# A recommendation tower on one core: a new order of each chunk's work on TensorE, ScalarE and VectorE

## The reference, cut to what matters

```python
e = jnp.stack([tbl_f[ids[:, f]] for f in range(26)], axis=1)      # 2048 x 26 x 128
combined = concatenate([dense[:, None, :], e], axis=1)            # 27 vectors of a sample
inter = einsum('bnd,bmd->bnm', combined, combined)[:, triu_i, triu_j]   # 351 products
h = concatenate([dense, inter, dense], axis=1)                    # 607 features
h = maximum(h @ W_top1 + b_top1, 0)                               # 512
h = maximum(h @ W_top2 + b_top2, 0)                               # 256
y = h @ W_top3                                                    # 2048 x 1
```

## Time and profile before

| | before |
|---|---|
| device time, median of 3 runs | 371.46 us |
| device time of the profiled execution | 371.68 us |
| its span | 369.8 us |
| TensorE busy with matmuls | 331.2 us (90%) |
| GpSimd busy | 259.1 us (70%) |
| VectorE busy | 208.4 us (56%) |
| ScalarE busy | 188.2 us (51%) |
| mean granted TensorE clock | 0.991 |

### The profile page before, as it was taken

How to read it: one execution, slowest core, us unless ns; L and a number is a source line. 1 busy time by engine, 2 the same in 40 slices (tenths; PEclk the granted TensorE clock), 3 DMA queues, 4 the chain that set the end, 5 groups by cost and what they waited for, 6 DMA issues and landing times.

```text
span 369.8 us, 13491 instructions
## 1 busy us (share of the span) xinstructions
PE 331.2 (90%) x6048; PEld 295.2 (80%) x6048; DVE 208.4 (56%) x376; ACT 188.2 (51%) x222; POOL 259.1 (70%) x280
## 2 busy tenths in 40 slices
PE   0486759899999999999999989998999989999797
PEld 0476747898899889997899769996889868997676
DVE  3799925792289506980398406980289505960031
ACT  2698643356355664556365554555445552555402
POOL 6777777777777777777777777777777777777100
PEclk9999998999999999999999999999999999999989
DMA  7999527672236512672247322572236512542330
GB/s 178 249 256 206 159 69 236 141 228 56 60 78 171 169 51 62 124 232 60 54 96 194 127 58 54 125 241 51 58 85 158 176 52 53 110 111 59 77 47 14
DMA packets 49332, 44.24 MB, mean 120 GB/s; under 512 B 33359, under 2 KB 39094, under 8 KB 49274
## 3 DMA queue, kind: packets, MB, share of 16 engines
q1 hardware_dynamic: 39166, 25.36, 27.4%
q0 software_dynamic: 8704, 17.84, 18.0%
q10 hardware_dynamic: 1404, 0.17, 0.3%
HBM read 37.91 MB, written 5.44 MB: 117 GB/s over the span
## 4 chain that ended last, share of the span: by engine, by line
PE 78%; DMA 8%; POOL 4%; issue 4%; SPq 2%; ACT 2%; DVE 0%; DVEq 0%
PE banks L449 37%; PE banks L472 13%; PE mlp L492 8%; PE moved L431 8%; PE mlp L502 7%; DMA hidden<-in_tbl_dram 6%; POOL rows L404 4%; DMA rows<-in_tbl_dram,ids_sb 3%; SPq L253 2%; PE banks L538 1%; PE mlp L514 1%; PE banks L552 1%; ACT vectors L866 1%; ACT vectors L849 1%; PE mlp L538 1%
## 5 line engine op out<-in xcount | busy, mean ns | idle before, releaser
L404 POOL DMA_INDIRECT rows<-in_tbl_dram,ids_sb x272 | 258.1, 949 | 83.9 <-issue 80.2
L711 DVE TENSOR_TENSOR masks<-hot_ids,row_of 125x512 fp32r<-125x512 int32 (+1 forms) x336 | 186.4, 619 | 59.9 <-PE banks L449 51.6
L449 PE MATMUL banks<-masks,high 125*128 125x256 f32 x592 | 152.4, 296 | 16.7 <-DVE low L698 16.7
L449 PE MATMUL banks<-masks,low 125*128 125x256 f32 x592 | 147.2, 287 | 0.0
L449 PEld LDWEIGHTS banks<-masks,high 125*128 125x128 f32 x592 | 115.6, 195 | 17.7 <-issue 14.6
L449 PEld LDWEIGHTS banks<-masks,low 125*128 125x128 f32 x592 | 115.9, 196 | 0.0
L866 ACT ACTIVATE vectors<-moved 128x512 f32<-128x512 f32 (+1 forms) x79 | 86.5, 1094 | 22.6 <-PE moved L431 22.6
L849 ACT ACTIVATE vectors<-banks 128x512 f32<-128x512 f32 (+1 forms) x40 | 44.4, 1110 | 70.4 <-PE banks L449 70.4
L472 PEld LDWEIGHTS banks<-vectors 128*27 128x27 f32 x4096 | 45.6, 104 | 22.6 <-issue 14.8
L472 PE MATMUL banks<-vectors 128*27 128x27 f32 x4096 | 56.3, 193 | 4.7 <-issue 3.7
L431 PE MATMUL moved<-identity,rows 128*128 128x128 f32 x271 | 45.0, 281 | 14.1 <-ACT vectors L866 6.4
(11 more groups left out here) (49 smaller groups left out, 65.4 us busy)
## 6 DMA issues: line engine op xcount, KB each, us to landing
hot_ids<-in_ids_of_field_dram SPq DMA_DIRECT2D x32, 256.0 KB, 4.7
rows<-in_tbl_dram,ids_sb POOLq DMA_INDIRECT x272
features<-scratch SPq DMA_DIRECT2D x7, 351.0 KB
scratch<-products SPq DMA_DIRECT2D x56, 42.2 KB
scratch<-products SPq DMA_DIRECT2D x28, 81.2 KB
w_sb<-in_tbl_dram SPq DMA_DIRECT2D x3, 448.0 KB
hot_ids<-in_ids_of_field_dram SPq DMA_DIRECT2D x8, 128.0 KB
dense_sb<-in_dense_dram SPq DMA_DIRECT2D x8, 128.0 KB, 5.3
```

Of the source, the lines that this page charges most:

```text
L404: pool.indirect_dma_start(rows[:, (tile * TILE_ROWS + v) % RING, :], None, tables[f][:, :], bass.IndirectOffsetOnAxis(ap=ids_sb[:, tile, f ...
L449: last = nc.tensor.matmul(banks[:, j % BANKS, m * CHUNK:(m + 1) * CHUNK], part[:, part_of(j * PAIR + m, k), :], masks[:, mask % MASK_RING, ...
L711: nc.vector.tensor_tensor(masks[:, mask % MASK_RING, 0:size], hot_ids[0:PART_ROWS, n % ID_RING, 0:size], row_of[0:PART_ROWS, row:row + 1]. ...
```

## The change

On TensorE a chunk now has this order: the turns of tile a stand between `look_up(i, 2)`, `look_up(i, 3)`, `look_up(i, 4)` and `first_layer(i-1, 0)`. Behind the last of them come steps 0 and 1 with the rest of the first layer and two turns of tile b, then the whole second layer, then `look_up(i+1, 0)` and the first two masks of `look_up(i+1, 1)` between the later turns of tile b, and last the visits of steps 2 and 3 with the rest of `look_up(i+1, 1)` between them. So two lookups of the next chunk, not one, run ahead of it. In `end` the last layers of chunk 6 stand ahead of the last turn, and two of half 0's four first-layer tiles stand between steps 2 and 3. ScalarE's and VectorE's queues are put in the matching order. On SyncE's queue the store of chunk 6's results moves ahead of the last writes.

The diff, with TensorE's part whole but for `first_chunk`, and the rest cut:

```diff
             def chunk(i):
-                a = TILES * i
+                a, b = TILES * i, TILES * i + 1
                 turn(a, 0)
-                look_up(i, 1)
+                look_up(i, 2)
                 last_layer(i - 2)
                 turn(a, 1)
-                look_up(i, 2)
+                look_up(i, 3)
                 turn(a, 2)
-                look_up(i, 3)
+                look_up(i, 4)
                 turn(a, 3)
-                look_up(i, 4)
+                first_layer(i - 1, 0)
                 turn(a, 4)
-                if i < LAST:
-                    end_of_chunk(i)
-
-            def end_of_chunk(i):
-                b = TILES * i + 1
-                first_layer(i - 1, 0)
+                if i == LAST:
+                    return
                 multiply(i, 0, (0,))
-                turn(b, 0)
                 first_layer(i - 1, 1)
                 multiply(i, 0, (1,))
-                turn(b, 1)
+                turn(b, 0)
                 first_layer(i - 1, 2)
                 multiply(i, 1, (0,))
+                first_layer(i - 1, 3)
+                multiply(i, 1, (1,))
+                turn(b, 1)
+                second_layer(i - 1, 0)
+                second_layer(i - 1, 1)
                 turn(b, 2)
-                first_layer(i - 1, 3)
+                look_up(i + 1, 0)
                 turn(b, 3)
-                multiply(i, 1, (1,))
-                second_layer(i - 1, 0)
+                look_up(i + 1, 1, range(0, 2))
                 turn(b, 4)
-                second_layer(i - 1, 1)
-                multiply(i, 2, (0,))
-                look_up(i + 1, 0, range(0, 3))
-                multiply(i, 2, (1,))
-                look_up(i + 1, 0, range(3, 5))
-                multiply(i, 3, (0,))
-                look_up(i + 1, 0, range(5, PARTS[0]))
-                multiply(i, 3, (1,))
+                products_of_second_tile(i)
+
+            def products_of_second_tile(i):
+                multiply(i, 2, (0,))
+                look_up(i + 1, 1, range(2, 4))
+                multiply(i, 2, (1,))
+                look_up(i + 1, 1, range(4, 6))
+                multiply(i, 3, (0,))
+                look_up(i + 1, 1, range(6, PARTS[1]))
+                multiply(i, 3, (1,))
...
             def end():
...
-                second_layer(LAST - 1, 0, range(2, MTILES1))
+                last_layer(LAST - 1)
                 turn(b, 4)
-                second_layer(LAST - 1, 1, range(0, 2))
                 multiply(LAST, 2)
-                multiply(LAST, 3)
-                second_layer(LAST - 1, 1, range(2, MTILES1))
-                last_layer(LAST - 1)
                 first_of_half(0, 0, every)
                 first_of_half(0, 1, every)
+                multiply(LAST, 3)
                 first_of_half(0, 2, every)
                 first_of_half(0, 3, every)
...
         # VectorE
                 make_masks(i, 0)
+                make_masks(i, 1)
                 place_dense(i)
-                make_masks(i, 1)
                 keep_dense(i - 1)
...
         # SyncE
             write_last(0)
             load_last(0)
+            store_y(LAST - 1)
             write_last(1)
-            store_y(LAST - 1)
             load_last(1)
```

More of the change, by code:

```diff
@@ L580, in end @@
                 multiply(LAST, 1, (1,))
+                turn(b, 1)
+                first_layer(LAST - 1, 3)
+                second_layer(LAST - 1, 0)
                 turn(b, 2)
[L582 to L583 removed]
+                second_layer(LAST - 1, 1)
                 turn(b, 3)
[L585 removed]
+                last_layer(LAST - 1)
                 turn(b, 4)
[L587 removed]
                 multiply(LAST, 2)
[L589 to L591 removed]
                 first_of_half(0, 0, every)
                 first_of_half(0, 1, every)
+                multiply(LAST, 3)
                 first_of_half(0, 2, every)
@@ L617, in first_chunk @@
                 turn(1, 1)
-                multiply(0, 0)
+                multiply(0, 0, (0,))
                 turn(1, 2)
-                multiply(0, 1)
+                multiply(0, 0, (1,))
                 turn(1, 3)
+                multiply(0, 1, (0,))
+                look_up(1, 0, range(0, 3))
+                multiply(0, 1, (1,))
+                look_up(1, 0, range(3, PARTS[0]))
                 turn(1, 4)
-                multiply(0, 2, (0,))
-                look_up(1, 0, range(0, 3))
@@ L625, in first_chunk @@
-                multiply(0, 2, (1,))
-                look_up(1, 0, range(3, 5))
-                multiply(0, 3, (0,))
-                look_up(1, 0, range(5, PARTS[0]))
-                multiply(0, 3, (1,))
-            def second_chunk():
-                turn(2, 0)
-                look_up(1, 1)
-                turn(2, 1)
-                look_up(1, 2)
-                turn(2, 2)
-                look_up(1, 3)
-                turn(2, 3)
-                look_up(1, 4)
-                turn(2, 4)
-                end_of_chunk(1)
+                look_up(1, 1, range(0, 2))
@@ L683, in _ @@
             pe.wait_ge(constants_made, CONSTANTS)
             first_chunk()
-            second_chunk()
-            for i in range(2, CHUNKS):
+            for i in range(1, CHUNKS):
                 chunk(i)
@@ L986, in chunk @@
             def chunk(i):
-                a = TILES * i
+                a, b = TILES * i, TILES * i + 1
                 keep_batch(a, 0)
-                keep_pair(i, 1)
+                keep_pair(i, 2)
                 keep_y(i - 2)
                 keep_batch(a, 1)
-                keep_pair(i, 2)
+                keep_pair(i, 3)
                 keep_batch(a, 2)
-                keep_pair(i, 3)
+                keep_pair(i, 4)
                 keep_batch(a, 3)
-                keep_pair(i, 4)
+                keep_first(i - 1, 0)
@@ L997, in chunk @@
                 keep_batch(a, 4)
-                if i < LAST:
-                    end_of_chunk(i)
-            def end_of_chunk(i):
-                b = TILES * i + 1
-                keep_first(i - 1, 0)
-                keep_batch(b, 0)
+                if i == LAST:
+                    return
                 keep_first(i - 1, 1)
                 keep_step(i, 0)
+                keep_batch(b, 0)
+                keep_first(i - 1, 2)
+                keep_first(i - 1, 3)
+                keep_step(i, 1)
@@ L1029, in end_of_last @@
                 keep_batch(b, 2)
-                keep_first(LAST - 1, 3)
+                keep_second(LAST - 1, 0)
                 keep_batch(b, 3)
-                keep_second(LAST - 1, 0)
             first_chunk()
-            second_chunk()
-            for i in range(2, CHUNKS):
+            for i in range(1, CHUNKS):
                 chunk(i)
```

40 lines of the change are left out of this document (13 added, 27 removed).

## The result

The changed kernel takes **398.88 us** (median of 4 runs, 395.53 to 400.89) against 371.50 us before: a ratio of 1.072 with a 95% interval of 1.069 to 1.075. It is slower by 27 us. The forecast was 397 us, slower, with a range of 384 to 410.

The account below looks back on a forecast made before the run. Gathers (42.6 us a chunk) bound the old kernel; the loop through DRAM, 14.3 + 30.2 = 44.5 us, would bind the new. With start and end the time was 391.3 us, plus 5.8 for low clock: 397 us, range 384 to 410.

Parts of the forecast that it names:

- loop through DRAM: Product step, drain, writes, load, first layer, next product step: claimed to set each chunk's cycle at 44.5 us.
- Rivals 1 and 4: 1: faster, gathers keep the lead, 370.6 us, chance 0.04; 4: no effect, time stays at 371.5 us, chance 0.02.
- rival 2: The way through DRAM stays hidden, the drain waits do not: cycle 42.85 us, time 381 us, chance 0.08.
- rival 3: All goes badly: 15.1 us for the way, low clock in all seven chunks; 407 us, with beyond chance 0.14.
- The way: Products through DRAM, from a chunk's last product step to the landed load: 14.3 us, within 13.5 and 15.1.
- The wait for the load: TensorE ahead of each chunk's first layer: 1.65 us a chunk, 0.85 to 2.45.
- (a): Step 0, right behind the turn of tile a's last batch, waits for ScalarE's drain: 1.0 us a chunk.
- (b): Chunk's end: a lookup's drain stands ahead of tile b's fourth batch's, so the next turn waits: 0.85 us.
- (c): Step 2 waits for ScalarE's drain of the last batch: 0.75 us a chunk.
- From the first layer to the next step 3: TensorE's stretch from first-layer start to the next chunk's last product step: 23.5 us before, 30.2 us after, drain waits included.
- The clock: TensorE at low clock behind waits: 4.2 us over half of seven chunks, plus 1.6 us at the end.
- The end: After the last load: 24.3 us to the last product step, half 0's load binding, then 10.2 and 7.7 us.

Follow-up runs that it names:

- x_way: Changed kernel, but in chunks 1 to 6 only half of the products are written to DRAM and loaded back, TensorE's instructions unchanged; 388.55 us.
- x_twice: Kernel before the change, but each chunk's products except the last's are written to DRAM twice before the load; 415.71 us.
- x_drain: Changed kernel with TensorE and ScalarE work reordered to remove its three waits for ScalarE's drains; 387.41 us.
- x_hold: Changed kernel with useless matmuls (5, 3, 4, 1 and 20) where TensorE waits, each filling meant to be shorter than its wait; 393.22 us.
- x_chunk: Changed kernel with the old end of the program, so only the chunks have the new order; 393.52 us.
- x_tail: Kernel before the change with only the new end of the program; 375.37 us.
- x_load: Changed kernel with half of the next chunk's second lookup moved behind the chunk's last product step; 391.03 us.
- x_even: Changed kernel reordered to remove the load wait and the three drain waits, with step visits and other work alternating; 381.01 us.
- x_both: Changed kernel with the edits of x_load and x_drain together; 382.13 us.
- x_best: Kernel before the change with another end: second-layer work between the last chunk's last two product steps; 370.44 us against 371.22, ratio 0.998.

## Why the prediction was right

**The bound.** Right. The loop through DRAM took the gathers' place in every chunk; x_way (a shorter way, same instructions) and x_twice (a longer one in the old order) show it from both sides. Rivals 1 and 4 fell with the waits for rows that never came back, rival 2 with the 9.8 us of waits for loads, and rival 3 needed 15.1 us of way and a low clock in every chunk.

**The way.** 14.3 us were taken, within 13.5 and 15.1. Measured from the end of step 3 to the first layer: 13.5 to 14.65 us, 14.0 on average. In the chain above the tile starts 0.04 us behind the landing.

**The wait for the load.** 1.65 us a chunk; measured 0.85 to 2.0, 1.40 on average, 9.8 us in seven. The way's excess over the 12.65 us of TensorE's work was the right sum.

**The waits for ScalarE.** (a) 1.0 was taken, 0.83 measured; (b) 0.85 and 1.1; (c) 0.75 and 0.51. Their sum, 2.4 us against 2.6, and their places are right, as the chain shows. In x_drain 2.0 us of them are gone in a chunk, and the cycle is 1.8 us shorter, with less waiting for the load and longer pauses in the steps: they lie on the path.

**From the first layer to the next step 3.** This is the term that was mis-sized: 30.2 us in the prediction, 31.6 measured on average (30.5 to 32.4). In x_hold, where the clock never fell in the profiled execution, it is 30.5. So 0.3 us were missing at full clock. What the six chunks have above x_hold's, 6.4 us in all, lies for some 4.5 us in the three chunks with the low clock, for which the prediction had a term of its own, and for 1.6 us in chunk 2, where the clock did not fall, but step 3 stands for 1.41 us without a cause that the profile names. The prediction had counted no such pause.

**The clock.** The size is right, the cause is half wrong. The prediction counted 4.2 us for the chunks and 1.6 for the end; x_hold measures 5.7 for all, the start included, for which nothing was foretold. Between the two profiled executions it is 4.2 us from the first step 3 to the last, 1.8 behind it and 2.0 ahead of it. That 4.2 is met so closely is partly luck, since the runs differ by as much. And the prediction laid the fall to the waits for the load, with (a) behind them. In the profiled execution the clock fell in three chunks, each time behind (b) and (c). These two waits in chunk 1, by TensorE's timeline, and the windows behind them (busy time of each engine; the granted clock is the third column from the right):

```profile
102.53 0.30 PE L431 MATMUL moved<-identity,rows 128*128 128x128 f32 x1 [1.08 <-ACT vectors L850]
103.34 1.00 PE L472 MATMUL banks<-vectors 128*27 128x27 f32 x64 [0.51 <-ACT vectors L850]
```

```profile
103.00:104.00 1.00, 0.66 (x56) 0.56 (x56) 0.48 (x1) 0.29 (x1) 0.70 (x2) 1.00 0.22 61
104.00:105.00 1.00, 1.00 (x12) 0.93 (x12) 0.00 (x0) 0.00 (x0) 0.70 (x2) 0.55 0.02 4
105.00:106.00 1.00, 1.00 (x7) 1.00 (x5) 0.46 (x1) 0.00 (x0) 0.69 (x2) 0.50 0.35 82
...
107.00:108.00 1.00, 1.00 (x28) 0.94 (x18) 0.08 (x1) 0.53 (x1) 0.83 (x1) 0.74 0.24 66
```

TensorE had stood for 1.08 us until 102.53 and 0.51 until 103.34; the clock is 1.00 until 104 and 0.50 behind it, with TensorE busy all the time. The load waits of 0.9 to 2.0 us drew no such stretch here. Elsewhere one did: in x_drain a load wait of 2.07 us, in x_chunk one of 2.45 us, while two of 2.09 and 2.10 us in x_chunk drew none; and x_drain's other two stretches came behind pauses of 1.78 and 1.69 us in the steps. So the fall does not belong to one kind of wait, and no run shows which wait will draw it: (b) and (c) stand in each of the chunks 1 to 6, and the clock fell in three of them. The changed kernel's times go with the clock: its four runs have mean clocks of 0.987, 0.974, 0.974 and 0.966 and take 395.5, 398.7, 399.1 and 400.9 us. The Trainium skill says on its page "TensorE: Matmul & The Clock Gate", in Part 1, that the number of matmuls that run slow differs from run to run of the same kernel; it speaks of a kernel's start. These four runs agree in that their mean clocks differ; where in each of them the clock fell, only the profiled one shows.

**The cycle and the sum.** 44.5 us, and 45.1 with the clock's 4.2 spread over seven chunks; measured 45.6. Step 3 of chunk 6 was foretold for 333.1 and came at 339.3: 0.4 us less at the start (65.7 for 66.1), 6.6 more in six cycles. Of these 6.6 the prediction had put 4.2 under the clock; the load landed 0.6 us earlier behind step 3. What is left over is 1.4 us, and the forecast missed the profiled execution by about as much (1.7). The bound of 386 is a slip: by the prediction's own terms it is 397.1 - 4.2 - 7 x 0.8 = 387.3.

**The end.** First layer to step 3: 24.3 us foretold, 24.3 measured, but not by the path that was foretold, so that this agreement is luck. The prediction let half 0's load bind, 21.2 us behind the start of the first layer, and put TensorE's own work up to the end of step 2 at some 20.5, "all off the path". In the trace the load goes out at 370.51 and no tile of half 0 waits for it; the chain stays with TensorE and the drains, step 2 ends at 373.60, 20.6 us in, and step 3 takes 1.75 us instead of 1.2 (x_tail shows the same). The 0.6 us that the bound came earlier made up for the slower step. Step 3 to half 1's reader: 10.2 and 10.2. The wait there: 4 us or more foretold, 5.07 measured. The rest: 7.7 and 1.6 of low clock, 9.3 measured. "No pause" was too much: 0.19 and 0.35 us are left of 1.96. That two tiles between them do not pay is what x_tail adds, and for a reason that the prediction had seen: TensorE then has nothing to do ahead of half 1.

## What to carry to other kernels

Under the loop that sets the time look for the next one, and write down by how much it is covered: here 2.3 us of cover lay over a way of 14 us through DRAM. A change that took 4 us of work out of that stretch, without adding an instruction, made TensorE wait there in every chunk, some 8 of the 27 us that were lost (x_load). A new neighbour on the engine that runs in order is a new wait, too: for each moved step count how long the draining engine needs for what stands ahead of it. And where an engine must wait, a short wait can cost twice, once as time and once as clock.

## What the runs showed of the hardware that was not expected

*The instruction flow.* Pauses that the profile puts down to nothing ("issue", in steps 0 to 3) were 2.9 us in the changed kernel, 5.2 in x_way (the same instructions on TensorE), 6.8 in x_load, 9.1 in x_drain, 9.4 in x_even and 11.7 in x_both: the fewer other waits there were, the more, and more where the steps' small matmuls stood together (x_both) than where most of them had other work between (x_even). From the start of step 2 to the end of step 3 the last chunk takes 4.5 us in the earlier trace rows, with nothing in between but the pause of 1.96 us, and 5.2 us in x_best with 2.0 us of other work in between and a pause of 0.48. The Trainium skill, page "Runtime: NRT & Kernel Launch", section "Instruction fetch mechanics", calls the cost of crossing from one block of instructions to the next mostly hidden; if these pauses are that cost, the row of x_both, 11.7 us, disagrees. That these pauses are the fetching itself is an inference from where they fall; no run here measures it apart.

*Work for nothing.* 13 useless matmuls a chunk and 20 at the end made the kernel 5.7 us faster (x_hold), with the granted clock at 1.0 in the profiled execution and 0.991 to 0.996 in the others, against 0.966 to 0.987; with 21 and 36 of them nearly all of it was lost again (x_fill, 398.06 us), though the clock was as high.

*A longer wait.* Behind 5.08 us of standing still a first-layer tile ran at the lower level from its start and took twice its time, 3.78 us (x_twice); behind waits of 1 to 2 us it mostly did not.
